# A gather of 784 indirect transfers: the wait ahead of each transfer is set to the third one before it, in place of a wait ahead of each pair

## What is computed

```python
edge_index = jnp.stack([src, dst])
x = _layernorm(x + _L0_gnn_ref(x, edge_index, ...))   # the layer of this change
x = _layernorm(x + _L1_gnn_ref(x, edge_index, ...))   # two graph convolutions
x = _layernorm(x + _L2_gnn_ref(x, edge_index, ..., 4))# four rounds of messages
x = _layernorm(x + _L3_gnn_ref(x, edge_index, ...))   # attention over edges, 8 heads

# in _L0_gnn_ref: every edge reads the rows of both its nodes
edge_features = jnp.concatenate([x[src], x[dst]], axis=1)
h = edge_features @ W1.T + b1
h = jax.nn.relu(_batchnorm(h, g1, be1))
h = h @ W2.T + b2
edge_updates = jax.nn.relu(_batchnorm(h, g2, be2))
x_out = jax.ops.segment_sum(edge_updates, dst, num_segments=x.shape[0])
```

## Time and profile before

| | |
|---|---|
| median of 3 runs | 4666.66 us |
| lowest and highest | 4658.91 and 4675.53 us |
| the profiled execution's own time | 4677.76 us |
| its span from first to last instruction | 4675.8 us |
| mean granted TensorE clock | 0.817 |
| indirect transfers (L637) | 784, issued from 80.5 to 1542.6 us |
| busy share of the span: TensorE, VectorE, ScalarE, GpSimd | 75%, 62%, 30%, 23% |

### The profile page before, as it was taken

One profiled execution on the slowest core, in us unless ns is written; L12 is line 12 of the kernel. 1 busy time (PEld: TensorE's weight loads), 2 busy tenths in 40 slices (PEclk: granted clock), 3 DMA queues, 4 the chain that ended last, 5 costly groups with the idle time before them and its releaser, 6 DMA issues. The chain is left out here.

```text
span 4675.8 us, 83038 instructions
## 1 busy us (share of the span) xinstructions
PE 3483.7 (75%) x19041; PEld 1627.4 (35%) x19142; DVE 2879.6 (62%) x3796; ACT 1415.7 (30%) x1952; POOL 1093.9 (23%) x1131
## 2 busy tenths in 40 slices
PE   3776666574889888888877775377789947769994
PEld 2332222252444466665443333122222212222222
DVE  6887767537444455551021113499889949979993
ACT  1123334400222222221011111111088821118880
POOL 3777777666444122120000001000000000000000
PEclk8988878867999899997979997555599955559996
DMA  2345555645999633334838882722033362213331
GB/s 61 115 149 175 185 185 204 211 143 198 350 360 363 234 114 109 101 90 100 251 82 190 187 192 51 133 56 49 21 125 119 112 100 51 54 31 117 125 101 27
DMA packets 808847, 657.35 MB, mean 141 GB/s; under 512 B 599017, under 2 KB 686184, under 8 KB 808516
## 3 DMA queue, kind: packets, MB, share of 16 engines
q1 hardware_dynamic: 677642, 361.12, 29.1%
q10 hardware_dynamic: 106050, 243.93, 15.1%
q0 software_dynamic: 25088, 51.43, 4.3%
HBM read 316.58 MB, written 196.24 MB: 110 GB/s over the span
## 5 line engine op out<-in xcount | busy, mean ns | idle before, releaser
L637 POOL DMA_INDIRECT gat<-a_table,gidx x784 | 908.2, 1158 | 498.9 <-issue 272.7
L1371 DVE CUSTOM_DVE_ANT_0 masked<-psum,mask 128x1564 bf16<-128x1564 f32 x400 | 698.8, 1784 | 176.8 <-ACT mask L937 118.1
L1713 PE MATMUL psum<-qp,kp 96*128 96x391 bf16 x1600 | 589.5, 523 | 285.6 <-DVE mx L1371 160.5
L1406 DVE SCALAR_TENSOR_TENSOR pw<-ex,c_full 128x1564 f32<-128x1564 f32 x400 | 680.8, 1781 | 50.3 <-ACT ex L964 31.5
L1459 PE MATMUL psum<-one_src,one_dst 128*128 x1968 | 471.8, 381 | 271.5 <-issue 153.4
L964 ACT ACTIVATE ex<-psum 128x782 f32<-128x782 f32 x800 | 610.0, 826 | 77.8 <-PE psum L1735 59.8
L1125 DVE TENSOR_SCALAR one_src<-iota_sub,src_low 128x800 f16 x984 | 383.2, 430 | 200.2 <-issue 99.6
L1511 PE MATMUL psum<-c_ring,hp 128*128 128x512 bf16 (+1 forms) x2064 | 422.5, 360 | 75.2 <-DMA c_ring<-c_parts 53.1
L1713 PEld LDWEIGHTS psum<-qp,kp 96*128 x1600 | 173.5, 128 | 701.1 <-issue 701.1
L1459 PEld LDWEIGHTS psum<-one_src,one_dst 128*128 x1968 | 201.0, 106 | 525.9 <-issue 458.2
L1744 PE MATMUL psum<-pw,vaug 128*32 128x391 f32 x3200 | 348.8, 508 | 29.8 <-DVE pw L1406 9.4
(11 more groups left out here) (331 smaller groups left out, 3520.1 us busy)
## 6 DMA issues: line engine op xcount, KB each, us to landing
c_full<-c_whole SPq DMA_DIRECT2D x80, 977.5 KB, 5.0
a_edges<-gat SPq DMA_DIRECT2D x196, 256.0 KB
a_in<-a_edges ACTq DMA_DIRECT2D x98, 512.0 KB
r_edges<-r ACTq DMA_DIRECT2D x98, 512.0 KB
r_in<-r_edges SPq DMA_DIRECT2D x98, 512.0 KB, 3.5
c_whole<-c_sum ACTq DMA_DIRECT2D x100, 400.0 KB
dst_bc<-dst_half ACTq DMA_DIRECT2D x98, 256.0 KB
c_parts<-c_hi ACTq DMA_DIRECT2D x100, 200.0 KB
```

The lines of the kernel that those rows point to most:

```text
L637: g.indirect_dma_start(gat[:, s, 2 * k * P:2 * (k + 1) * P], None, a_table, bass.IndirectOffsetOnAxis(ap=gidx[:, s, k:k + 1], axis=0)).the ...
L1371: v.tensor_tensor_reduce(out=masked[:, n % 2, :].rearrange("p (c t) -> p c t", c=4), in0=psum[:, o:o + 4 * BANK].rearrange("p (c t) -> p c ...
L1406: v.scalar_tensor_tensor(pw[:, step_slot(k), :].rearrange("p (h t) -> p h t", h=HQ), ex[:, step_slot(k), :].rearrange("p (h t) -> p h t", ...
L1713: last = t.matmul(bank((n % 2) * 4 + c, CW), kp[0:KQK, n // 2, ds(b * P, P)], qp[0:KQK, n // 2, ((n % 2) * 4 + c) * CW:((n % 2) * 4 + c + ...
```

## The change

An indirect transfer n is issued when transfer n-3 has landed, whether n is even or odd. The eight semaphores are given to the transfers in turn (transfer n has number n mod 8) in place of one to each pair, and SyncE waits for the four semaphores of a group in place of two.

```diff
+UNDER_WAY = 3
 ...
             with sp.Fori(0, NG // 4) as i:
                 for s in range(4):
-                    for half in range(2):
-                        sp.wait_ge(gathered[2 * s + half], 32 * i + 32)
+                    for k in range(4):
+                        sp.wait_ge(gathered[(4 * s + k) % 8], 32 * i + 16 * (s // 2) + 16)
                     sp.dma_start(a_edges[ds(4 * i + s, 1)].rearrange("o p e -> (o p) e"),
                                  gat[:, s, :]).then_inc(a_staged[s], 16)
 ...
                     for k in range(4):
-                        if k % 2 == 0 and (s or not isinstance(i, int)):
-                            hold("pool", pool, gathered[(2 * s + k // 2 - 2) % 8], 32 * i + (32 if s else 0))
+                        n = 4 * s + k - UNDER_WAY
+                        if n >= 0 or not isinstance(i, int):
+                            hold("pool", pool, gathered[n % 8], 32 * i + 16 * (n // 8) + 16)
                         g.indirect_dma_start(gat[:, s, 2 * k * P:2 * (k + 1) * P], None, a_table,
                                              bass.IndirectOffsetOnAxis(ap=gidx[:, s, k:k + 1], axis=0)
-                                             ).then_inc(gathered[2 * s + k // 2], 16)
+                                             ).then_inc(gathered[(4 * s + k) % 8], 16)
```

## The result

The change made the kernel slower: 4708.9 us in the median of six runs (4697.5 to 4713.1) against 4662.2 us for the kernel before in six runs, a ratio of **1.0089, 95% interval 1.0068 to 1.0110**. The two medians are 47 us apart; 0.89% of the time before is 41 us, because the ratio isn't the quotient of the medians. Medians and ranges in this text take all runs, while the ratios leave out those more than 1.5% above the fastest of their kernel. The prediction was 4673 us with a range from 4655 to 4697. The profiled execution after took 4701.4 us, its span is 4699.7 us; the one shown of before took 4677.8 us and was, as now appears, 16 us above the median of its kernel.

The account below looks back on a forecast made before the run. Pass 1 was taken as paced by DMA, with the gather's 36 us delay nearly hidden in 24 us of slack: 13 - 4 - 3 = 6 us later, 4666.7 + 6, so 4673 us, range 4655 to 4697.

Parts of the forecast that it names:

- What bounds the kernel: Pass 1 is paced by DMA; the gather's staging ends 23.8 us before ScalarE's queue comes to the last load.
- given back: End of pass 1: slower gather leaves DMA time worth 4 us, quicker landings while ScalarE is held up about 3 us.
- the rival's 2.32 us a transfer: Gather in pass 1: upper bound if landing takes as long with three under way as with four; chance 0.30.
- Which waits are new: GpSimd's gather: only odd transfers wait anew, for n-3; 392 waits added, none taken away, four under way become three.
- holds cost nothing: GpSimd's queue: 392 more holds, at most 4 us over the gather, taken as 0.
- SyncE's two waits: SyncE, each group: two more waits; even 0.1 us more shows only at the last group, inside the slack.
- The counting stage: Up to 1158 us: new waits on some odd transfers cost 10 us, or 6 transfers more left for pass 1.
- Pass 1: Gather beside pass 1 slows from 2.10 to 2.22 us a transfer; last issue ends near 1580 us.
- the landing time doesn't give way at all: Rival for pass 1: 2.32 us a transfer, 25 us later, 4692 us; chance 0.30.
- The ring share: Rival for pass 1: landing time gives way entirely, 2.10 us a transfer stays, 4667 us; chance 0.15.
- What is late next: End of pass 1: last staging 13 us after ScalarE's queue reaches the last load; 6 us later after what is given back.
- Faster: Rival: later gather moves up to 1.4 MB into idle DMA time after 1544 us; pass 1 ends 4 us earlier, 4663 us; chance 0.10.

Follow-up runs that it names:

- e1: The kernel before, unchanged, profiled once more in the first group; ratio 0.993 (0.989 to 0.997) to the kernel before.
- fourth group: Changed kernel and four under way, unaltered, and both kernels with pass 1 put off by products on VectorE; ratios 0.9879 to 1.0221 to the kernel before.
- e12: The kernel before, unchanged, for a third profile; median 4646.1 us, ratio 1.002 (0.999 to 1.005).
- e13: The changed kernel, unchanged, once more; median 4710.3 us, ratio 1.0086 (1.0063 to 1.0109) to the kernel before.
- e4: The changed kernel's eight semaphores and SyncE's four waits, with the order of the pairs; ratio 0.987 (0.981 to 0.992) to the kernel before.
- e9: The kernel before (pairs), gather started only when 24 of 100 windows are counted; median 4870.5 us, ratio 1.049 (1.046 to 1.052).
- e10: The changed kernel (three under way), gather started only when 24 of 100 windows are counted; median 4904.0 us, ratio 1.054 to the kernel before.
- e15: The kernel before with 28 more products on VectorE in the stage of sums; median 4734.8 us, ratio 1.0142 (1.0114 to 1.0171).
- e16: The changed kernel with 28 more products on VectorE in the stage of sums; median 4775.5 us, ratio 1.0221 to the kernel before.
- e2: The changed kernel, unchanged, profiled once more in the first group; ratio 0.999 (0.994 to 1.004) to the kernel before.
- e6: The changed kernel (three under way) with half of the counting left out; 4620 us (4607 to 4647).
- e14: The changed kernel with four under way for every transfer in place of three; median 4613.1 us, ratio 0.9879 to the kernel before.
- third group: Pairs, three and four under way with the gather started late on purpose, and the kernel before unchanged; medians 4870.5, 4904.0, 4802.5 and 4646.1 us.
- second group: Pairs, three, four and six under way, each with half of the counting left out; 4631, 4620, 4656 and 4751 us.
- e17: The kernel before with pass 1 put off by 70 more copies on ScalarE in the stage of sums; ratio 1.0377 (1.0332 to 1.0423).
- e18: The changed kernel with pass 1 put off by 70 more copies on ScalarE in the stage of sums; ratio 1.0394 to the kernel before.

## Why the prediction was wrong

**What bounds the kernel: the step that failed.** "So the gather has 23.8 us of slack at its end" was read rightly from the execution shown and was no property of the kernel. Its counting stage had taken 797 us. In e1 the same program took 843 us for it, and the gather was done with some 155 us to spare; in the profile after the change and in all eight of the third and fourth group it took 718 to 722 us. Pass 1 then starts near 1084 us with 538 to 576 transfers issued in place of 600, catches up with the gather, and the slack is 0.2 us (e12, e13 and after). Everything that the prediction hid in the slack came to the surface. Without the slack its own sum reads: 36 us later, hardly anything given back, 4662 + 36 = 4698 us, just outside its range, against 4709 us measured. With the rival's 2.32 us a transfer it would be 55 us later (1599 - 1544), so the measured 47 us lie between the two.

Luck stands beside this. Between the two profiles the end of pass 1 moved by 5 us, where 6 were forecast, but only because the counting stage of the one before was 75 us longer. And 19 of the 24 us between those two executions fell behind pass 1, where the gather is over. The rest of the kernel behind pass 1 took 3077 to 3099 us in the profiles of the pairs and 3076 to 3096 us in those of the changed kernel and of four under way, so this is mostly the spread of executions.

**Which waits are new**, and that holds cost nothing: right as far as the pace shows it. The bookkeeping with the order of the pairs keeps their pace (e4, 2.14 us, against 2.09 to 2.14 us without it). No cost of SyncE's two waits was seen.

**The counting stage**, 10 us or 6 transfers: right in size where it was measured best. With the same late start it was 5 transfers (405 against 400 issued, e9 and e10), though the waits were frequent, 64.7 us in 89 pieces from 100 to 850 us after the change; most of them took the place of other idle time. With the ordinary start one profile of each says less: on the chip of the fourth group 457 transfers were issued by 928 us with the pairs (e15), 455 and 442 with three (e13, e16). A good part of this spread is something the prediction hadn't seen: ahead of 400 us a few issues take 4 to 20 us each, 5 of them or 38 us in e15, 6 or 52 us in e16, and 3 or 31 us in e13.

**Pass 1**, 2.22 us a transfer: mis-sized. It measured 2.27 to 2.35 us (after, e2, e6), so the upper bound of 2.32 was the right value: the landing gave way by next to nothing. The rival that was given 0.30 for this ("the landing time doesn't give way at all") was right in mechanism and in sign; its 25 us were too few by the 24 us of slack that it too relied on, and the two together, 49 us, are near the 47 measured. Four under way confirm it from the other side, 1.79 to 1.81 us against 1.74. The ring share, by which three under way keep the pace of four, fell with it (2.27 to 2.35 us against 1.79 to 1.81). The Trainium skill, "DMA: Bandwidth & Descriptors", section "Queues, rings and completion order", says that an engine goes round the rows that have work packet by packet; no run here contradicts that, but it doesn't follow that three under way are served at the rate of four, if at 6 us of landing the ring runs empty between them, an explanation that wasn't tested.

**What is late next**: right in place, ScalarE's load and the relu behind it, and wrong in extent, ten gaps of 113 us together (the profile puts them down to "issue") in place of one.

**Faster, by a later gather in idle DMA time**: not seen. What an earlier gather gives is larger: pass 1 fell from 525 to 433 us from three to four under way (e13, e14).

Not settled: how large the loss is to 10 us. By the medians it is 47 us in the first measurement, 36 us in the fourth group (e13) and 33 us with the late start; by the ratios the first two agree, 41 and 40 us. In the third group both kernels with a wait for each transfer, three and four under way, took 3087 to 3088 us behind pass 1 and the pairs 3078 us (e9), so up to 10 us of a loss may not be the gather's; one profile of each doesn't settle it. The ratio of e4, 0.987, is left unexplained too: its six runs lay within 12 us while the kernel before spread over 100 us in the same group, and it wasn't run again. So what the bookkeeping costs in time was never measured by itself.

## What to carry to other kernels

A slack between two chains that run side by side is a difference of two long times; before a cost is hidden in it, ask what sets each of them and whether it was the same in another execution. Here the profiled one stood at the top of its kernel's runs (4677.8 against 4658.9 to 4675.5), which was the warning. For transfers issued under a limit of three or four under way, the pace here was (issue + landing) / n; take the landing from the same stretch of the trace and don't count on a shorter one while the gather is a small part of the traffic. One more under way than in the changed kernel took 97 us off the time, as long as the gather was the bound. More isn't always better: six under way sped the gather up and yet gave the slowest kernel of the second group, for a cause that stays open. Put more work on VectorE to delay something only after looking at what GpSimd does meanwhile.

## What the runs showed of the hardware

**The counting stage is uneven by execution and chip, and the queues' short instructions go with it.** Its length went from 721 to 843 us for the unaltered kernel before (e12, e1) and from 718 to 900 us over all kernels that count in full, along with the granted TensorE clock (0.89 to 0.91 over 100 to 850 us in the short ones, 0.81 to 0.87 in the long ones). In the long ones instructions of VectorE's and TensorE's queues that usually take some 20 to 250 ns now and then take 0.7 us each. One line of VectorE's queue from 131 to 850 us, before and then after (minimum, median and maximum in ns):

```profile
L341 DVEq FUSED_REGOPS  x87: 4/244/721, 151.3 to 845.3; - x87
```

```profile
L342 DVEq FUSED_REGOPS  x98: 244/244/252, 151.0 to 843.2; - x98
```

Counted over VectorE's whole queue from 130 to 850 us, instructions of 0.55 to 0.9 us were 21 to 28 in the stages of some 720 us, every one of them a TENSOR_LOAD, and 108 to 161 in those of 796 to 900 us, where only 14 to 28 were TENSOR_LOADs. With half of the counting left out there were 216 to 268, and the stage took 728 to 826 us. None stood in the stretch from 1700 to 2100 us, but for 12 and 8 in e17 and e18, where pass 1 reached into it. What they wait for, the runs don't show, nor whether they lower the clock or go with it.

**GpSimd's issue of an indirect transfer is held up beside VectorE's f32 products**: 3.2 us in place of 0.95 us beside 3.5 us products (e15), and in the kernel before one of 4.21 us at 1036.2 us, beside a product of 3.5 us. Beside the reciprocal of 20 us in the same stage of e15 the issues stay at 0.94 to 0.97 us.

**Landing of an indirect transfer of 64 KB under full DMA engines**: from the end of its issue to the issue that waited for it 5.9 to 6.1 us with three under way (3 x 2.27 to 2.35, less 0.95) and 6.2 to 6.3 us with four (4 x 1.79 to 1.81, less 0.95).
